# A graph network on one core: V's half of the weighting on GpSimd, and a new order of TensorE's matmuls in graph attention

## The reference, cut to what matters

```python
def gat_conv(x, W, al, ar, b, src, dst):
    h = (x @ W).reshape(N, H, D)
    el = jnp.einsum('nhd,hd->nh', h, al)
    er = jnp.einsum('nhd,hd->nh', h, ar)
    e = jax.nn.leaky_relu(el[src] + er[dst], NEG_SLOPE)
    m = jax.ops.segment_max(e, dst, num_segments=N)
    ex = jnp.exp(e - m[dst])
    s = jax.ops.segment_sum(ex, dst, num_segments=N)
    alpha = ex / s[dst]
    out = jax.ops.segment_sum(alpha[:, :, None] * h[src], dst, num_segments=N)
    return jax.nn.elu(out.reshape(N, H * D) + b)
```

## Time and profile before

| | us |
|---|---|
| median of 3 runs (2108.72 to 2109.53) | 2108.91 |
| the profiled execution, its own time | 2108.91 |
| its span, first to last instruction | 2107.1 |
| VectorE busy | 1575.6 (75%) |
| ScalarE busy | 1379.3 (65%) |
| TensorE matmuls busy | 1724.7 (82%) |
| GpSimd busy | 274.3 (13%) |

### The profile page before, as it was taken

The page is one execution under the profiler, slowest core; times in us unless marked ns, Lnnn a source line. Parts: engine busy times, 40 slices in busy tenths (PEclk is TensorE's granted clock), DMA queues, the critical chain, the costliest instruction groups (busy, mean ns, idle before and its releaser), DMA issues. The chain is left out here.

```text
span 2107.1 us, 63497 instructions
## 1 busy us (share of the span) xinstructions
PE 1724.7 (82%) x21987; PEld 1375.5 (65%) x21987; DVE 1575.6 (75%) x3485; ACT 1379.3 (65%) x2350; POOL 274.3 (13%) x421
## 2 busy tenths in 40 slices
PE   3999995598999748899893699998989985588883
PEld 1333333598888627889882477775558984588883
DVE  6999997899999888999999532222332257899996
ACT  0246794999999659999995622221113355799986
POOL 2466510366700000000000000000000000000000
PEclk9999997799999978999996899999999998799997
DMA  2000000011101000010101200000001010000002
GB/s 77 12 1 2 2 3 27 14 31 37 40 27 40 2 27 30 28 40 28 40 28 50 97 2 0 0 0 7 0 16 40 20 61 14 8 27 21 21 21 99
DMA packets 34789, 54.87 MB, mean 26 GB/s; under 512 B 10668, under 2 KB 26240, under 8 KB 34432
## 3 DMA queue, kind: packets, MB, share of 16 engines
q1 hardware_dynamic: 31232, 51.64, 7.5%
q0 software_dynamic: 3328, 0.06, 0.1%
HBM read 43.19 MB, written 8.49 MB: 25 GB/s over the span
## 5 line engine op out<-in xcount | busy, mean ns | idle before, releaser
L1069 ACT ACTIVATE Rm<-rows,cB 128x1280 bf16<-128x1280 f32 (+3 forms) x816 | 847.1, 1132 | 32.4 <-DVE Mn L1104 19.2
L1206 PE MATMUL ps<-R,M 128*128 128x132 f16 (+1 forms) x8640 | 684.1, 221 | 117.3 <-DVE Mn L1104 62.7
L1206 PEld LDWEIGHTS ps<-R,M 128*128 128x128 f16 x8640 | 545.4, 97 | 141.6 <-DVE M L1114 51.8
L1114 DVE TENSOR_TENSOR M<-Rm,C 128x1280 f16<-128x1280 bf16 (+3 forms) x816 | 527.9, 673 | 37.0 <-ACT Rm L1069 26.6
L1199 PE MATMUL ps<-HB,C 128*128 128x66 f16 x6400 | 304.2, 194 | 60.5 <-DVEq L1095 60.5
L1199 PEld LDWEIGHTS ps<-HB,C 128*128 128x128 f16 x6400 | 258.9, 98 | 60.7 <-DVEq L1095 60.7
L600 PE MATMUL acc<-ohc,ohl 128*128 128x420 f16 (+1 forms) x1161 | 246.0, 348 | 27.1 <-DVE ohl L564 23.9
L562 DVE TENSOR_SCALAR ohc<-cells,near 128x1280 f16<-128x1280 f16 x387 | 214.7, 555 | 27.9 <-PE acc L600 23.5
L1117 DVE SCALAR_TENSOR_TENSOR M<-rows,cN,C 128x1280 f16<-128x1280 f32 (+1 forms) x144 | 217.2, 1508 | 0.0
L600 PEld LDWEIGHTS acc<-ohc,ohl 128*128 128x128 f16 x1161 | 89.6, 98 | 175.6 <-DVE ohl L564 120.0
L1543 PE MATMUL psA<-R,C 128*128 128x512 f16 (+1 forms) x800 | 145.6, 332 | 8.1 <-DVEq L1827 3.2
(11 more groups left out here) (295 smaller groups left out, 2304.9 us busy)
## 6 DMA issues: line engine op xcount, KB each, us to landing
rows<-rowd SPq DMA_DIRECT2D x32, 640.0 KB, 3.9
rows<-rowd SPq DMA_DIRECT2D x16, 320.0 KB, 3.4
xd<-R SPq DMA_DIRECT2D x4, 640.0 KB, 2.9
xr<-xd SPq DMA_DIRECT2D x20, 128.0 KB, 2.1
xd<-HB SPq DMA_DIRECT2D x1, 2560.0 KB
xr<-xd SPq DMA_DIRECT2D x5, 512.0 KB, 6.4
R<-in_x SPq DMA_DIRECT2D x1, 2432.0 KB
xr<-in_x SPq DMA_DIRECT2D x19, 128.0 KB, 2.0
```

Of the source, the lines that this page charges most:

```text
L1069: a.activation(Rm[:, s % SG, 0:wide(p)], rows[:, p % 2, 0:wide(p)], ACT.Relu, bias=cB[:, ds(h + s * nh, 1)]).then_inc(s_R, 1)
L1114: v.tensor_tensor(M[:, u, 0:wide(p)], Rm[:, u, 0:wide(p)], Cs, ALU.min).then_inc(s_M if s in ONE else s_cut, 1)
L1206: m = pe.matmul(region(p % 2, r), lhsT, rhs, start=split and opens and r % 3 == 0, stop=True, skip_group_check=True)
```

## The change

In the weighting phase `weighted` is replaced by `side`, which makes one of the two weights for a pair of tiles in one tensor_tensor. VectorE runs `side` for U (w = 0), GpSimd for V (w = 1), each for all ten pairs; both wait for the ring F by themselves (s_lo), GpSimd first for the factors (a new semaphore s_fac) and for its own constants. `high` waits for both (s_F and the new s_FV). U and V become two tensors instead of the two columns of one. In the main phase, the ten matmuls that don't need M are no longer issued ahead of the wait: the wait comes first, and then M's and C's matmul follow each other region by region.

```diff
-                    def weighted(v, k):
-
+                    def side(eng, k, w, q, s_done):
+
+                        Fv = F[:, k % 3, :, :].rearrange("p t (h w c) -> p (t h) w c", w=2, c=cw)
+                        Ht = HV[:, 2 * k:2 * k + 2, :, :].rearrange("p t h c -> p t (h c)").rearrange("p t (h c) -> p t h c", c=cw)
+                        qt = q[:, 2 * k * nh:(2 * k + 2) * nh]
                         if k >= 3:
-                            v.wait_ge(s_lo, k - 2)
-                        for t in (2 * k, 2 * k + 1):
-                            Ft = F[:, k % 3, t % 2, :].rearrange("p (h w c) -> p h w c", w=2, c=cw)
-                            Ht = HV[:, t, :, :].unsqueeze(2).to_broadcast([P, nh, 2, cw])
-                            q = weights[:, t * nh:(t + 1) * nh, :].unsqueeze(3).to_broadcast([P, nh, 2, cw])
-                            v.tensor_tensor(Ft, Ht, q, ALU.mult).then_inc(s_F, 1)
+                            eng.wait_ge(s_lo, k - 2)
+                        eng.tensor_tensor(Fv[:, :, w, :].rearrange("p (t h) c -> p t h c", t=2), Ht,
+                                          qt.rearrange("p (t h) -> p t h", t=2).unsqueeze(3).to_broadcast([P, 2, nh, cw]),
+                                          ALU.mult).then_inc(s_done, 1)
...
                         g.memset(HV[:, :, :, dh], 1.0).then_inc(s_one, 1)
+                        g.wait_ge(s_one, 2)
+                        g.wait_ge(s_fac, 1)
+                        for k in range(PAIRS):
+                            side(g, k, 1, V, s_FV)
...
+                        v.sem_inc(s_fac, 1)
...
-                            weighted(v, k)
+                            side(v, k, 0, U, s_F)
                             if k:
                                 low(k - 1)
...
                         def high(k):
-                            a.wait_ge(s_F, 2 * k + 2)
+                            a.wait_ge(s_F, k + 1)
+                            a.wait_ge(s_FV, k + 1)
...
-                                    Cd = lambda d: C[:, s * NP + p * W + d * P:][:, 0:P]
-                                    opens = s == 0
-                                    sides = lambda r: (r % 2, r // 2) if split else (0, r)
+                                    cut(pe, q, s, lambda eng, sem, value: eng.wait_ge(sem, value))
                                     for r in range(RG):
-                                        side, d = sides(r)
+                                        first = s == 0 and r % 3 == 0
+                                        side, d = (r % 2, r // 2) if split else (0, r)
+                                        lhsT = (Mn if side and s in TWO else M)[:, s % SG, d * P:(d + 1) * P]
+                                        rhs = UV[:, s, :, ds(h * (2 * cw) + side * cw, XW)]
+                                        m = pe.matmul(region(p % 2, r), lhsT, rhs, start=first, stop=True,
+                                                      skip_group_check=True)
                                         if split and side and s in TURNED:
-                                            pe.matmul(region(p % 2, r), Cd(d), VS[:, TURNED.index(s), :, ds(h * cw, cw)],
-                                                      start=False, stop=True, skip_group_check=True)
+                                            m = pe.matmul(region(p % 2, r), C[:, s * NP + p * W + d * P:][:, 0:P],
+                                                          VS[:, TURNED.index(s), :, ds(h * cw, cw)], start=False, stop=True,
+                                                          skip_group_check=True)
                                         if not split:
                                             both = region(p % 2, r).rearrange("p (l c) -> p l c", l=2)
-                                            pe.matmul(both[:, :, cw:2 * cw], Cd(d), VP[:, s, :, ds(h * cw, cw)],
-                                                      start=opens and r % 3 == 0, stop=True, skip_group_check=True)
-                                    cut(pe, q, s, lambda eng, sem, value: eng.wait_ge(sem, value))
-                                    for r in range(RG):
-                                        side, d = sides(r)
-                                        lhsT = (Mn if side and s in TWO else M)[:, s % SG, d * P:(d + 1) * P]
-                                        rhs = UV[:, s, :, ds(h * (2 * cw) + side * cw, XW)]
-                                        m = pe.matmul(region(p % 2, r), lhsT, rhs, start=split and opens and r % 3 == 0, stop=True,
-                                                      skip_group_check=True)
+                                            m = pe.matmul(both[:, :, cw:2 * cw], C[:, s * NP + p * W + r * P:][:, 0:P],
+                                                          VP[:, s, :, ds(h * cw, cw)], start=False, stop=True,
+                                                          skip_group_check=True)
                                     m.then_inc(s_P, 1)
```

More of the change, by code:

```diff
@@ L827, in attention @@
                 with Phase() as ph:
-                    weights = ph.sb("weights", [P, TH, 2], f32)
-                    U, V = weights[:, :, 0], weights[:, :, 1]
+                    U, V = ph.sb("U", [P, TH], f32), ph.sb("V", [P, TH], f32)
                     XC, tt = ph.sb("XC", [P, TH], f32), ph.sb("tt", [P, TH], f32)
@@ L841, in attention @@
                     psM, psB = ph.ps("psM", [nh + 1, P]), ph.ps("psB", [P, nh + 1])
-                    s_vp, s_v, s_top, s_turn, s_dg, s_all, s_e, s_ex, s_one, s_F, s_hi, s_lo = (
-                        ph.sem(n) for n in ("vp", "v", "top", "turn", "dg", "all", "e", "ex", "one", "F", "hi", "lo"))
+                    s_vp, s_v, s_top, s_turn, s_dg, s_all, s_e, s_ex, s_fac, s_one, s_F, s_FV, s_hi, s_lo = (
+                        ph.sem(n) for n in ("vp", "v", "top", "turn", "dg", "all", "e", "ex", "fac", "one", "F", "FV", "hi", "lo"))
                     block = ph.enter_context(nc.Block())
@@ L929, in _ @@
                         v.wait_ge(s_ex, 4)
-                        ch(v.tensor_scalar(U, U, kap[:, 0:1], None, ALU.mult))
-                        ch(v.tensor_scalar(V, V, kap[:, 0:1], 1.0 if split else -1.0, ALU.mult, ALU.mult))
+                        ch(v.tensor_scalar(U[:, :], U[:, :], kap[:, 0:1], None, ALU.mult))
+                        ch(v.tensor_scalar(V[:, :], V[:, :], kap[:, 0:1], 1.0 if split else -1.0, ALU.mult, ALU.mult))
                         ch.wait()
                         if split:
-                            turned = V.rearrange("p (a b h) -> p a b h", b=5, h=nh)[:, :, 1:4:2, :]
+                            turned = V[:, :].rearrange("p (a b h) -> p a b h", b=5, h=nh)[:, :, 1:4:2, :]
                             ch(v.tensor_scalar(turned, turned, -1.0, None, ALU.mult))
                             ch.wait()
+                        v.sem_inc(s_fac, 1)
                         def low(k):
@@ L956, in _ @@
                         a.wait_ge(s_e, 1)
-                        a.activation(U, XC[:, :], ACT.Exp).then_inc(s_ex, 1)
-                        a.activation(V, XC[:, :], ACT.Exp, scale=SLOPE).then_inc(s_ex, 1)
+                        a.activation(U[:, :], XC[:, :], ACT.Exp).then_inc(s_ex, 1)
+                        a.activation(V[:, :], XC[:, :], ACT.Exp, scale=SLOPE).then_inc(s_ex, 1)
                         a.activation(F12[:, 0, :], tt[:, :], ACT.Exp).then_inc(s_ex, 1)
```

## The result

Slower: 2120.99 us (median of 5 runs, 2118.68 to 2123.28) against 2108.91 (5 runs, 2108.72 to 2110.32), ratio 1.0056 with a 95% interval of 1.0041 to 1.0072. That is +12.1 us, where +27.5 was forecast. The sign is right and the time lies inside the wide range (2116 to 2152 us), but it is outside the forecast's own range (2130 to 2145), and the size is less than half.

The account below looks back on a forecast made before the run. VectorE was taken to bound the weighting loops and to lead TensorE in layer 0's main phases; 2108.9 + 26.3 - 0.3 + 1.5 = 2136.4 us, own range 2130 to 2145 (0.67), 8-in-10 range 2116 to 2152.

Parts of the forecast that it names:

- One line of three operations: Weighting loops: GpSimd's read can't run while VectorE's does, so a pair's three operations stand in one line, 3.3 us.
- the sum of the loop: Weighting: a pair costs 3.3 us, ten pairs 33.0 in place of 24.2; three loops +26.3 us.
- GpSimd's price: Weighting: GpSimd's 528-column multiplication costs 1.1 to 1.46 us, taken as 1.3.
- Full durations for a beat: Weighting: VectorE's operations counted at 0.70 and 1.25 us, because neighbours' overlap is lost where GpSimd comes between.
- only the copy's price: Rival, weighting: GpSimd needs 0.63 to 0.85 us, +6 to +13 in three loops, 2116 to 2123 us; chance 0.07.
- The -0.3 us in the sum: A term of -0.3 us in the forecast total; its derivation is not in the text given.
- TensorE's order: Main phases: C's matmuls coming behind the wait for M cost +1.5 us together, 0.6 to 5.
- The end of the phase: End of layer 0's two attentions: nothing covers C's ten matmuls, 2 x 0.31 = 0.6 us.
- the start: Start of layer 0's main phases: first ten matmuls behind M, mostly covered; 2 x 0.2 = 0.4 us, at most 1.5.
- The borders: Between parts: ScalarE's evacuation up to 0.31 us later, mostly absorbed by its 4.6 us waiting; 0.5 us, at most 3.
- Layer 3: Main phase of layer 3: VS matmuls stand in steps needing M alone, made ahead; the new order costs nothing.

Follow-up runs that it names:

- in turns: Kernel before plus declared bounds and the new weighting, GpSimd's multiplication and VectorE's operations made to alternate; 2176.34 us, against 2120.28 with only the bounds.
- GpSimd writes only: Kernel before plus declared bounds and the new weighting, GpSimd's multiplication replaced by a constant memset (results wrong); 2105.49 us, against 2120.28 with only the bounds.
- TensorE's order alone: Kernel before plus declared bounds and only the new matmul order, weighting as before; 2125.26 us, against 2120.28 with only the bounds.
- behind the wait but not mixed: Kernel before plus declared bounds, C's ten matmuls moved behind the wait, after M's ten in a row; 2123.38 us, against 2120.28 with only the bounds.
- GpSimd's part alone: Kernel before plus declared bounds and only the new weighting, matmul order as before; 2125.62 us, against 2120.28 with only the bounds.
- GpSimd twice: Kernel before plus declared bounds and the new weighting, each GpSimd multiplication done twice, matmul order as before; 2154.21 us, against 2120.28 with only the bounds.

## Why the prediction was right and wrong

**One line of three operations: right, and now shown in both directions.** The rows of before had shown only GpSimd standing still behind VectorE. The profile after shows VectorE behind GpSimd (2.12 us for L945 in place of 1.25), each of GpSimd's operations run twice gives one more stretch of 0.87 us for one more operation, and where GpSimd only writes there is none (0.70 and 1.25 us). So in these loops the two engines don't meet only at semaphores.

**The step that failed is the sum of the loop: 0.70 + 1.25 + 1.3 + 0.05 us of full durations for a pair.** The mechanism was right and this term was mis-sized: +26.3 us forecast for the three loops, +9.2 measured. A pair takes 2.66 us and not 3.3. It is too large in two ways.

*GpSimd's price.* I took 1.3 us, it is 1.07 undisturbed (run in turns). The row it came from, L489 of 1.11 us, held 0.26 us of standing still behind L572, if it stood still as L856 does. I had seen that, by the mechanism on which I built everything, and still placed the price between the disturbed and the undisturbed reading. The undisturbed one, 1.8 ns a column and 1.1 us for 528, was right; (1.07 - 0.17)/528 is 1.7 ns. The price was 0.23 us a pair too high.

*Full durations for a beat.* This is the larger part, 0.41 us a pair. I said that neighbours' overlap is lost where GpSimd comes between. It isn't: GpSimd's operation of 1.07 adds 0.87 to the pair's 2.66 us, and what is left for VectorE's own two is 0.62 + 1.17 = 1.79 us, as before. Where GpSimd writes only, they follow each other at 1.78 us (379.45 to 381.23). So 0.48 us too much for GpSimd, 0.23 of it by the price, and 0.16 for VectorE, 0.64 a pair, 19 us in thirty pairs. With the right price of 1.07 alone the sum would still have been 3.07 us a pair and +19 us for the three loops, over twice the 9.2 measured. Ten pairs at 2.66 are +2.5 us, the weighting took +3.1; the remainder lies at the loop's start and end.

**The time inside the wide range was luck.** The range reached down to 2116 us for the sake of the rival *only the copy's price* (2116 to 2123), and the measured 2121 us lies in it. But that rival is refuted: GpSimd needs 1.07 us and not 0.63 to 0.85. What it adds to the line, 0.87, happens to be nearly the rival's number.

**The -0.3 us in the sum: no run shows this term.** It was not worked out from any row. In the first attention the four exponentials take 0.34, 0.32, 0.32 and 0.32 us and the two scalings 0.30 each in the kernel before, with U and V at every second column, and the same in the kernel after, with U and V at unit stride.

**TensorE's order: right in its places, three times too small.** Forecast +1.5 (0.6 to 5), measured 5.3 alone and 5.0 in the kernel after, at the edge. The end of the phase costs 0.3 us each, as I had it, and the start nothing, where I had put 0.2 each. The borders are the rest, some 2.3 us in each phase, where I had put 0.5 for both: I let ScalarE's 4.6 us of waiting for M absorb them. Those waits are seven in number, one in two parts, 0.7 us, and they are still there, 4.6 us, in the kernel after: so they were no slack that could take up a delay. That ScalarE waits there for a VectorE which the late evacuation has delayed as well is my reading, argued and not tested. The rows fit it: ScalarE's wait of 0.66 us ends 33.1 us behind the start of the last read-out that the change delays, in both kernels (454.74 to 487.87 before, 455.69 to 488.81 after), so the wait moved along and didn't shrink. A delay of the evacuation of 0.24 us went through in full, 0.29 us in each two parts.

**Layer 3: right.** Its main phase is 264.1 to 265.4 us in all kernels, with either order.

**The whole time** adds up by stages to +13.4 us, where the medians differ by 12.1. The kernel before ran between 2107.7 and 2112.5 us over all its executions, the kernel after between 2118.7 and 2123.3. In code that both share, the start is 2.6 us shorter and the rest 2.5 us longer in the one profile of each, so the two cancel in the sum. The prediction had neither. The first comes with GpSimd's multiplications; what makes the second isn't settled.

## What to carry to other kernels

Before an elementwise half goes to GpSimd, ask what it costs VectorE while it runs: here, beside VectorE's tensor_tensor and scalar_tensor_tensor with two SBUF inputs each, the half cost 0.87 us in the line where it had cost 0.62 on VectorE. If a duration is to be a price, take it from a row in which the mechanism under discussion wasn't at work, and put overlapping neighbours into the sum by start-to-start spacing, not by duration (here 1.79 us and not 1.95 for VectorE's two). Work that doesn't need the operand waited for belongs ahead of the wait above all in the last step before someone else's read-out (here that step alone cost the whole 2.6 us of a main phase), and an engine's waiting for a partner is no slack until it is seen to shrink when the engine is late (ScalarE's 4.6 us were the same before and after). Read the stages that a change doesn't touch as well: here one of them moved by 2.6 us.

## What the runs showed of the hardware that was not expected

- VectorE's instruction is stretched by less (0.87 us: 2.12 against 1.25, kernel after) than the GpSimd operation it stands behind lasts (1.07 us undisturbed, run in turns). So some 0.2 us of the two overlap, an estimate from these numbers; which part of them is not shown.
- GpSimd's memset of 528 columns, 0.55 us (379.59 to 380.14, GpSimd writes only), ran fully inside VectorE's two-input tensor_tensor (379.45 to 380.15), which kept its 0.70 us.
- TensorE alternated matmuls of 132 and 66 columns into overlapping places of PSUM at the same pace as in two runs of ten: 0.89 us for a step of twenty, both ways (457.82 to 458.71 with TensorE's order alone, 458.31 to 459.20 behind the wait but not mixed).
- With two declared bounds on values loaded from a table, the stretch up to the first weighting, in which they are read, was 11 us longer (368.0 against 356.8 us, one profile each).
- With multiplications for GpSimd later in the program, its first IOTA started at 3.1 us in four kernels (after, GpSimd's part alone, in turns, GpSimd twice); in the ten others it started at 9.9 to 10.6 us.
